# The mixer's output projection as three float32r products, with the residual stream in DRAM and buffers shared

## What is computed

```python
g = y * jax.nn.silu(gate)
gg = g.reshape(b, s, G, INTER // G)
var = jnp.mean(gg * gg, axis=-1, keepdims=True)
gg = gg * jax.lax.rsqrt(var + EPS)
out = gg.reshape(b, s, INTER) * norm_w
return jnp.einsum('bsi,oi->bso', out, out_proj_w)
...
x = x + _L0_attn_a_ref(_layernorm(x, axis=-1), ...)
```

## Time and profile before

| | us |
|---|---|
| median of 3 runs | 2751.22 (2750.11 to 2752.27) |
| the profiled execution | 2748.32 |
| its span in the profile | 2746.5 |
| mean granted clock | 0.967 |

### The profile page before, as it was taken

The page is one execution under the profiler, slowest core; times in us unless marked ns, Lnnn a source line. Parts: engine busy times, 40 slices in busy tenths (PEclk is TensorE's granted clock), DMA queues, the critical chain, the costliest instruction groups (busy, mean ns, idle before and its releaser), DMA issues. The chain is left out here.

```text
span 2746.5 us, 42314 instructions
## 1 busy us (share of the span) xinstructions
PE 2537.2 (92%) x14144; PEld 1770.3 (64%) x14144; DVE 1924.8 (70%) x3759; ACT 1452.7 (53%) x3497; POOL 392.4 (14%) x448
## 2 busy tenths in 40 slices
PE   3579999999999999999999999996989889999799
PEld 2467777777776777776777677764874534444488
DVE  5367878777787787787877887865556467676354
ACT  2265656556657566566666565643223346666311
POOL 2101111111111111110110110122220011111121
PEclk7799999999999999999999999998999989999899
DMA  2322232223223223223323223212013111110000
GB/s 91 97 59 65 66 90 67 62 69 89 64 61 97 63 68 90 59 71 88 67 65 88 67 64 84 68 26 88 0 74 124 66 47 41 36 40 25 1 12 19
DMA packets 195003, 172.68 MB, mean 63 GB/s; under 512 B 31264, under 2 KB 157296, under 8 KB 193136
## 3 DMA queue, kind: packets, MB, share of 16 engines
q1 hardware_dynamic: 189344, 168.13, 22.3%
q10 hardware_dynamic: 5456, 2.00, 0.3%
HBM read 151.70 MB, written 18.38 MB: 62 GB/s over the span
## 5 line engine op out<-in xcount | busy, mean ns | idle before, releaser
L487 PE MATMUL bank<-xh,wh 128*128 128x512 f32 x1152 | 467.4, 406 | 49.4 <-DVE wl L838 33.6
L694 ACT ACTIVATE xch<-bank,pk 128x64 f32<-128x64 f32 x1024 | 219.9, 360 | 530.0 <-PE bank L569 528.9
L617 PE MATMUL bank<-wo,yt 128*128 128x512 f32 x1024 | 452.1, 594 | 16.7 <-issue 13.8
L487 PE MATMUL bank<-xl,wh 128*128 128x512 f32 x1152 | 452.3, 393 | 0.0
L487 PE MATMUL bank<-xh,wl 128*128 128x512 f32 x1152 | 452.2, 393 | 0.0
L812 DVE SCALAR_TENSOR_TENSOR cacc<-raw,cwh,cacc 128x512 f32<-128x512 f32 x480 | 360.5, 751 | 44.4 <-ACT cacc L796 32.9
L617 PEld LDWEIGHTS bank<-wo,yt 128*128 128x128 f32 x1024 | 192.9, 190 | 238.1 <-issue 235.3
L487 PEld LDWEIGHTS bank<-xh,wh 128*128 128x128 f32 x1152 | 218.4, 190 | 97.6 <-DVE wl L838 34.4
L487 PEld LDWEIGHTS bank<-xh,wl 128*128 128x128 f32 x1152 | 218.1, 189 | 47.7
L487 PEld LDWEIGHTS bank<-xl,wh 128*128 128x128 f32 x1152 | 218.7, 190 | 40.3
L2043 ACT ACTIVATE at_PT<-bank 128x512 f32<-128x512 f32 (+3 forms) x384 | 167.4, 498 | 118.3 <-PE bank L1958 113.8
(11 more groups left out here) (246 smaller groups left out, 4637.6 us busy)
## 6 DMA issues: line engine op xcount, KB each, us to landing
xn<-w_hs_dram SPq DMA_DIRECT2D x112, 256.0 KB, 2.7
EC<-ecum_scratch SPq DMA_DIRECT2D x112, 256.0 KB, 8.6
xn<-w_gate_dram SPq DMA_DIRECT2D x80, 256.0 KB, 3.0
wo<-w_out_dram SPq DMA_DIRECT2D x8, 2048.0 KB, 9.1
rawx<-w_gate_dram SPq DMA_DIRECT2D x48, 256.0 KB, 3.1
rawx<-w_hs_dram SPq DMA_DIRECT2D x48, 256.0 KB, 2.7
qk_scratch<-at_part SPq DMA_DIRECT2D x48, 256.0 KB
at_qT<-qk_scratch SPq DMA_DIRECT2D x32, 192.0 KB, 2.6
```

Source lines behind the costliest of these rows:

```text
L487: mm = nc.tensor.matmul(BA[bank][:, :], w[:, s, k, :], x[:, k, tok], start=(k == 0 and m == 0), stop=(k == KC - 1 and m == 2))
L617: mm = nc.tensor.matmul(BA[b][:, :], yt[:, j * P:(j + 1) * P], wo[:, j, :], start=(j == 0), stop=(j == JT - 1))
L694: o = nc.scalar.activation(xch[:, hh * HP:(hh + 1) * HP], BT[1 - u][:, i * HP:(i + 1) * HP], ACT.Copy, scale=pk[:, h, c, O_DT + hh:O_DT + ...
```

## The change

- In the mixer the output projection is three float32r products for each of 8 slices: yh x woh, yh x wol, yl x woh. ACT casts yt to `yh` after yt x gate, ahead of the square; DVE forms `yl` = yt - yh after its first fold. yl shares yt's memory, so it also waits for the square.
- The weights: ACT's scaling by norm_w now writes a float32r `woh`; DVE forms `wol` = wo * nw - woh in eight operations in slot 0 of each group, spread between its conv and silu steps, in wo's memory. PE's projection waits for all eight and for yl.
- `sq` lies in `sg`'s memory; the square waits for the slot's second gate tile on DVE, a gate tanh for the sum of squares of the slot before.
- x isn't kept in SBUF during the mixer. SP loads one 128-row tile of it per slot into `xz` (two buffers), DVE adds to it there, SP stores it to `x_scratch` in DRAM. After the mixer SP stores the last tile, waits for it, and reads all of x back into `xr` ahead of the FFN's weights.
- `SHARE` is (0,3), (3,7), (7,10), (10,10): 3 conv tiles in slots 0 and 4, 4 in slots 1 and 5.

The core of the diff:

```diff
-        SHARE = [(0, 4), (4, 7), (7, 10), (10, 10)]
+        SHARE = [(0, 3), (3, 7), (7, 10), (10, 10)]
...
-        wo = sb(ctx, "wo", [P, JT, C])
+        wo, wol = shared("wo", [P, JT, C])
+        woh = sb(ctx, "woh", [P, JT, C], F32R)
...
-        yt = sb(ctx, "yt", [P, GC])
+        yt, yl = shared("yt", [P, GC])
+        yh = sb(ctx, "yh", [P, GC], F32R)
         sg = sb(ctx, "sg", [P, GC])
+        sq = sg[:, :].rearrange("p (j t) -> p j t", j=JT)
+        xz = sb(ctx, "xz", [P, 2, C])
...
-            pe.wait_ge(wo_set, 17 * g + 17)
...
-            dv_gg.wait(pe, n + 1)
+            dv_wo.wait(pe, JT * (g + 1))
+            dv_yl.wait(pe, n + 1)
             for j in range(JT):
-                mm = nc.tensor.matmul(BA[b][:, :], yt[:, j * P:(j + 1) * P], wo[:, j, :], start=(j == 0), stop=(j == JT - 1))
+                for m, (y, w) in enumerate(((yh, woh), (yh, wol), (yl, woh))):
+                    mm = nc.tensor.matmul(BA[b][:, :], y[:, j * P:(j + 1) * P], w[:, j, :],
+                                          start=(j == 0 and m == 0), stop=(j == JT - 1 and m == 2))
...
             dv_gg.wait(act, n + 1)
+            nc.scalar.copy(yh[:, :], yt[:, :]).then_inc(ac_yh.sem, 1)
+            if step:
+                dv_sg.wait(act, gates_done(n, 1))
             pe_ss.wait(act, n)
-            nc.scalar.activation(sq[:, :, :], yt[:, :].rearrange("p (j t) -> p j t", j=JT), ACT.Square).then_inc(ac_sq.sem, 1)
+            nc.scalar.activation(sq, yt[:, :].rearrange("p (j t) -> p j t", j=JT), ACT.Square).then_inc(ac_sq.sem, 1)
...
+        def dv_y_low(dve, n):
+
+            ac_yh.wait(dve, n + 1)
+            ac_sq.wait(dve, n + 1)
+            nc.vector.tensor_tensor(yl[:, :], yt[:, :], yh[:, :], ALU.subtract).then_inc(dv_yl.sem, 1)
+
+        def dv_out_low(dve, g, i):
+
+            for j in (2 * i, 2 * i + 1):
+                ac_wo.wait(dve, JT * g + j + 1)
+                nc.vector.scalar_tensor_tensor(wol[:, j, :], wo[:, j, :], nw[:, 0, j:j + 1], woh[:, j, :],
+                                               ALU.mult, ALU.subtract).then_inc(dv_wo.sem, 1)
...
             dv_fold(dve, n, 0)
+            dv_y_low(dve, n)
+            dv_fold(dve, n, 1)
             if not last:
                 dv_masked(dve, *nxt, (1,))
-            dv_fold(dve, n, 1)
...
+            low(0)
             conv(0)
+            low(1)
             conv(1)
             silu(0)
+            low(2)
             if not last:
                 dv_masked(dve, *nxt, (2, 3))
+            low(3)
             conv(2)
...
+            dve.wait_ge(d_xin[n % 2], 16 * (n // 2 + 1))
+            nc.vector.scalar_tensor_tensor(xz[:, n % 2, :], BA[b][:, :], rr[:, 1:2], xz[:, n % 2, :], ALU.mult, ALU.add)\
...
+                def load_x(n):
+
+                    if n >= 8 * G:
+                        return
+                    if n >= 2:
+                        sp.wait_ge(d_xout[n % 2], 16 * (n // 2))
+                    src = A["x"] if n < NT else x_dram
+                    sp.dma_start(xz[:, n % 2, :], src[n % NT * P:(n % NT + 1) * P, :]).then_inc(d_xin[n % 2], 16)
+
+                def store_x(n):
+                    dv_out.wait(sp, n + 1)
+                    sp.dma_start(x_dram[n % NT * P:(n % NT + 1) * P, :], xz[:, n % 2, :]).then_inc(d_xout[n % 2], 16)
...
                     if z < NT - 1:
                         next_decay(g, z)
+                    if z > 0:
+                        store_x(8 * g + z - 1)
...
+                    if 0 < z:
+                        load_x(8 * g + z + 1)
...
                     load_out(sp, g + 1)
                     load_pack(g + 1, 1)
+                    store_x(8 * g + 7)
+                    load_x(8 * g + 9)
...
+                sp.dma_start(xr[:, 0, :], x_dram[0:P, :]).then_inc(s_xr[0], 16)
+                sp.dma_start(xr[:, 1:, :], x_dram[P:, :].rearrange("(z p) c -> p z c", p=P)).then_inc(s_xr[1], 16)
                 sp.dma_start(wr[:, :, :], A["gate_w"]).then_inc(s_w, 16)
```

More of the change, by code:

```diff
@@ L83, in build @@
     skip_dram = nc.dram_tensor("skip_scratch", [P, G, JT], F32).ap()
+    x_dram = nc.dram_tensor("x_scratch", [T, C], F32).ap()
     qk_dram = nc.dram_tensor("qk_scratch", [2, AH, SK, T], BF16).ap()
@@ L95, in sem @@
             return top.enter_context(nc.semaphore(name))
-        xr = sb(top, "xr", [P, NT, C])
         ident = sb(top, "ident", [P, P])
@@ L108, in build @@
         turned = sem(top, "turned")
-        mixer(nc, A, xr, ident, identb, nhalf, stat, mv, rstd, xn, BANK, pack_dram, rows_dram, ecum_dram, skip_dram, sb, sig, sem, turned, debug)
+        mixer(nc, A, x_dram, ident, identb, nhalf, stat, mv, rstd, xn, BANK, pack_dram, rows_dram, ecum_dram, skip_dram, sb, sig, sem, turned, debug)
+        xr = sb(top, "xr", [P, NT, C])
         wgu = sb(top, "wgu", [P, KC, 2, F])
@@ L116, in build @@
         s_w, s_wd = sem(top, "d_ffn"), sem(top, "d_ffn_down")
+        s_xr = [sem(top, f"d_residual{i}") for i in range(2)]
         with nc.Block() as block:
@@ L123, in build @@
         SG = {}
-        FW = (wgu, wd, wr, s_w, s_wd)
+        FW = (wgu, wd, wr, s_w, s_wd, s_xr)
         ffn(nc, A, FW, SG, xr, ident, nhalf, stat, mv, rstd, xn, BANK, sb, sig, sem, "f1")
@@ L145, in _, with mixer @@
                 sp.wait_ge(s, 16)
-def mixer(nc, A, xr, ident, identb, nhalf, stat, mv, rstd, xn, BANK, pack_dram, rows_dram, ecum_dram, skip_dram, sb, sig, sem, turned, debug):
+def mixer(nc, A, x_dram, ident, identb, nhalf, stat, mv, rstd, xn, BANK, pack_dram, rows_dram, ecum_dram, skip_dram, sb, sig, sem, turned, debug):
     with ExitStack() as ctx:
@@ L157, in mixer, with shared @@
         LAST_TILE = STEPS * NTILE
+        def shared(name, shape):
+            with nc.sbuf_tensor(name, shape, F32) as whole:
+                pass
+            return whole, sb(ctx, name + "_lo", shape, F32R)
         xh = sb(ctx, "xh", [P, KC, T], F32R)
@@ L188, in mixer @@
         with ExitStack() as c0:
+            xr = sb(c0, "x0", [P, NT, C])
             xnT = sb(c0, "xnT", [P, KC, T])
@@ L431, in mixer @@
             ctx, "pe_P", "pe_small", "pe_hs", "pe_diff", "pe_yoff", "pe_ydiag", "pe_state", "pe_ss", "pe_out")
[L432 to L435, removed]
+        (ac_hi, ac_tail, ac_raw, ac_th, ac_xc, ac_ex, ac_tg, ac_yh, ac_sq, ac_wo) = sig(
+            ctx, "ac_hi", "ac_tail", "ac_raw", "ac_tanh", "ac_xdt", "ac_exp", "ac_gate", "ac_yhi", "ac_sq", "ac_wo_hi")
+        (dv_lo, dv_cv, dv_act, dv_sm, dv_M, dv_yo, dv_yd, dv_sg, dv_gg, dv_yl, dv_wo, dv_st, dv_out, dv_r, dv_sq) = sig(
+            ctx, "dv_lo", "dv_conv", "dv_silu", "dv_small", "dv_M", "dv_yoff", "dv_ydiag", "dv_gate", "dv_gg", "dv_ylo", "dv_wo_lo", "dv_state", "dv_out", "dv_r", "dv_sq")
         (po_cw, po_xd, po_s1, po_r) = sig(
@@ L442, in mixer @@
         d_rw, d_ec = sem(ctx, "d_rw"), sem(ctx, "d_ec")
+        d_xin = [sem(ctx, f"d_xin{i}") for i in range(2)]
+        d_xout = [sem(ctx, f"d_xout{i}") for i in range(2)]
         RAW, TAP = 3, TAPS - 1
@@ L678, in ac_gate_tanh @@
             dv_sg.wait(act, m - 1)
+            pe_ss.wait(act, (m - JT) // 2)
             pe_P.wait(act, q + 1)
@@ L696, in ac_xdt, with ac_out_high @@
             o.then_inc(ac_xc.sem, 1)
-        def ac_weigh(act, g, i):
-            act.wait_ge(wo_set, 17 * g + 16)
+        def ac_out_high(act, g, i):
+            act.wait_ge(wo_set, 16 * g + 16)
             act.wait_ge(d_pk[0], 48 * g + 48)
             for j in (2 * i, 2 * i + 1):
-                o = nc.scalar.activation(wo[:, j, :], wo[:, j, :], ACT.Copy, scale=nw[:, 0, j:j + 1])
-            if i == JT // 2 - 1:
-                o.then_inc(wo_set, 1)
+                nc.scalar.activation(woh[:, j, :], wo[:, j, :], ACT.Copy, scale=nw[:, 0, j:j + 1]).then_inc(ac_wo.sem, 1)
         def ac_relu(act, g, z, q):
@@ L734, in weigh @@
                 if z == 0:
-                    ac_weigh(act, g, i)
+                    ac_out_high(act, g, i)
             if not last:
@@ L930, in dv_slot, with low @@
             dv_fold(dve, n, 0)
+            dv_y_low(dve, n)
+            dv_fold(dve, n, 1)
             if not last:
                 dv_masked(dve, *nxt, (1,))
-            dv_fold(dve, n, 1)
+            def low(i):
+                if z == 0:
+                    dv_out_low(dve, g, i)
             def conv(r):
@@ L1051, in load_rows @@
                                      rows_dram[side, :, bass.ds(g * HG, HG), z * P:(z + 1) * P]).then_inc(d_rw, 16)
+                def load_x(n):
[8 more added lines that the diff above has]
+                    sp.dma_start(x_dram[n % NT * P:(n % NT + 1) * P, :], xz[:, n % 2, :]).then_inc(d_xout[n % 2], 16)
+                load_x(0)
+                load_x(1)
                 sp.wait_ge(s_set, 3)
@@ L1112, in _ @@
                     load_pack(g + 1, 1)
+                    store_x(8 * g + 7)
+                    load_x(8 * g + 9)
                 for z in range(NT):
                     slot_loads(G - 1, z, True)
+                store_x(8 * G - 1)
```

(16 more changed lines are left out.)

2 lines of the change are left out of this document (removed).

## The result

| us | before | after |
|---|---|---|
| median | 2751.6 (2750.11 to 2752.27) | 2867.51 (2865.74 to 2870.25) |
| profiled execution | 2748.32 | 2868.35 |
| its span | 2746.5 | 2866.5 |
| mean granted clock | 0.967 | 0.935 |

The ratio is 1.0423 (95% interval 1.0405 to 1.0441): the change makes the kernel 4.2% slower. The forecast was 2860, from 2805 to 2910.

The account below looks back on a forecast made before the run. PE was taken to bound the mixer's middle. Terms -48.5 + 24.7 + 27.2 + 44.8 + 11.3 + 41.6 + 8.5 = +109.6 us on 2748.3 gave 2857.9, put at 2860 for the median; range 2805 to 2910.

Parts of the forecast that it names:

- The product: Output projection: 24 float32r products at conv tiles' pace, 5.56 us for 6.87, -1.31 us a slot if PE never waits.
- the rival of 2705: Projection products run at the skill's 131 ns, 3.1 us for 24, giving 2705 us; chance 0.01.
- The new wait: PE's projection waits for yl, or wol in slot 0: pauses of 4.4, 5.2 and 8.6 us in slots 3, 7, 0.
- The moved tile: A conv tile moves from slot 0 to slot 1, where PE is the bound, at 2.78 us, in 8 groups.
- The clock: Projections after new pauses run at lower granted clock: 1.60 us in each of 26 slots, +41.6 us.
- The rival in which the clock holds: Granted clock holds through PE's pauses of 4 to 8 us: 2818 us; chance 0.12.
- The residual: Residual x in DRAM: 0 inside the mixer, +8.5 us before the FFN's first cast, bounds 2 and 10.6.
- The rival that DVE is late: DVE's added work delays slots with conv tiles through late weight splits; the 37 gains go, 2908 us; chance 0.06.

Follow-up runs that it names:

- e2_share: The changed kernel with only the old `SHARE` of conv tiles put back (4 in slots 0 and 4, 3 in slots 1 and 5): 2845.39 us.
- e1_fill: The changed kernel with unused float32r products issued just before PE's new waits, so that PE is busy in the pauses: 2820.62 us.
- e8_loads: The changed kernel with slot 1's x load moved into slot 0 and all but x's first 128 rows loaded behind the FFN's weights: 2862.8 us.
- e5_slot0: The changed kernel with products reordered by operand, the fourth tile back in slot 0, and ACT's weighing and DVE's low halves moved earlier there: 2735.67 us.
- e7_all: e5_slot0 plus e8_loads' moves, ACT's cast earlier in slots without conv tiles, and DVE's subtraction before its first fold: 2705.66 us.
- e9_share: e7_all with one line changed, the fourth conv tile moved from slot 0 back to slot 1: 2701.87 us.

## Why the prediction was right

**The product.** Predicted -1.31 us a slot; slots 2 and 6 gained 1.39. The pace of the conv tiles held: the 24 products of slots 1 and 2 span 5.67 us to the end of the last one, where the 16 float32 instructions took 7.03. The distance of two products at full clock is 0.23 us (298.69 to 298.92 in slot 3). The Trainium skill's figure of about 131 ns ("TensorE: Matmul & The Clock Gate", section "Back-to-back issue gap"), and the rival of 2705 with it, is not borne out by these rows.

**The new wait.** Slot 3 4.23 us for 4.40, slot 7 5.04 for 5.20, slot 0 9.04 for 8.6. Slots 4 to 6 of the last group paused 4.04 for 4.20, and its slot 7 6.76 for the 6.77 of the prediction (2.87 and 3.90). All chains were put together from single lengths and distances of before, in the order that the diff writes. Slot 0 was longer by the low halves: two take 1.32 us (427.07 to 428.39), not 1.20, and there are four pairs.

**The moved tile.** 22.2 us, from half of two tiles' 5.56; slot 1 of e2_share gave 21.8, and its whole time 22.1.

**The clock.** Right in kind, its size a little small: 1.60 a slot was predicted, from the one pause in the profile that had cost something, and e1_fill gave back 1.7. Slots 3 and 7 mostly lost 1.4 to 1.8 (projections of 7.06 to 7.43 us against 5.67), slot 0 1.8 to 2.6 (7.49 to 8.27). The rival in which the clock holds had 2818; that is the kernel that e1_fill made of it, 2821.

**The residual.** FFN's first product came 32.0 us after the end of the last sums of squares (1988.14 to 2020.15), where it had been 24.6 (1879.72 to 1904.33): +7.4 for +8.5. Inside the mixer it was taken at 0; the table and e8_loads leave nothing for it, though the bound was drawn too low: the stores landed after 8.8 us (median of 64), not 2.0.

**Not foreseen.** From the FFN's first product to the end of the span the same work took 846.4 us for 842.2; the first FFN has 2.7 of that (142.1 for 139.4). Windows of PE in after, just behind the FFN's start:

```profile
2026.00:2034.00 8.00, 6.90 (x35) 1.00 0.00 0
2034.80:2041.60 6.80, 6.80 (x23) 0.50 0.00 0
2042.00:2050.00 8.00, 8.00 (x45) 1.00 0.00 0
```

Half the clock for 6.8 us, in a stretch where PE had been busy; at the like place of before (1918.8 to 1925.6) it was granted 1.00. All ten kernels with x in DRAM have such a fall, of 3.4 or 6.8 us, between 14.6 and 17.0 us after the FFN's first product, and first FFNs of 140.9 to 142.9 us; the kernel before has none. Why it falls there was not settled. The rest of the 4.2 us does not recur: in the nine other kernels the whole stretch took 841.1 to 844.2 us. The mixer's last sums moved by 108.4 (1879.22 to 1987.64), where the prediction's terms for it make 101.1: the first slot of all accounts for 3.4 of it (its projection ended 7.8 later, 210.54 to 218.36, not 4.4; 2.0 of that stood ahead of the slot's first gate product, 182.20 to 184.24, and from 180 to 184 us the granted clock was 0.50, in before 0.90), groups 3 and 6 for 3.7, the last group for 0.9 (26.2 for 25.3), and the others took back 0.7. With +4.2 behind the FFN's start and -1.1 at it that makes the 10.4 us by which the profiled execution, 120.0 longer, exceeded the sum of 109.6.

**The rival that DVE is late** had 0.06 and didn't come in after, where PE's pauses hid it; it came in e5_slot0 and e7_all, once they were gone: in slot 1, behind DVE's last operation of slot 0, and through the weight splits only for 2.2 and 3.2 us.

## What to carry to other kernels

Before a product is split, ask which of its parts needs which operand, and issue the parts in the order in which their operands come: here the same 24 products are 125 us apart by order alone. Cheaper work gains only in the slots where something covers the new chain, so sort the slots by what stands between the chain's first link and the consumer, and price the uncovered ones, with the slow products that follow a pause, by themselves. When a wait is taken away, count the load of the other engines in that slot first, since the next one may be only 2 us behind.

## What the runs showed of the hardware

- Idle time of PE costs more than itself: in or just after each of 27 pauses of 3.7 to 9.1 us the granted clock fell to 0.50, which cost a further 46 us, and unused products in them gave it back (e1_fill). Shorter pauses cost it only at times: it fell in 3 of the 8 slots 1 of e7_all (pauses of 2.7 us), in 3 of the 8 slots 0 of e9_share (1.7 to 1.9 us) and in none of those of the kernel before (1.7 us).
- The granted clock fell to 0.50 for 6.8 us at 2034.8 in after, 14.6 us after PE had begun the FFN's products and while it was busy; the nine other kernels with x in DRAM show the same, for 3.4 or 6.8 us.
- A float32r product of 128 x 128 by 128 x 512 with its own weight load passes each 0.23 us at full clock (298.69 to 298.92), and 0.42 at half (295.50 to 295.92).
- A 256 KB store landed after 2.0 us (median of 8, the kernel's last) in the kernel before and after 8.8 us (median of 64) in after, where loads stand around it in SP's queue; what makes it longer was not tested.
